# Gate and up of a feed-forward layer by Strassen's identity: seven block products in place of eight

## The chip, the cores and the metric

The kernel runs on one core of one Trainium2 chip. A core has TensorE (PE in the rows: matrix products, SBUF to PSUM), VectorE (DVE), ScalarE (ACT), GpSimd (POOL) and SyncE (SP, which issues most DMAs); each works through its own instructions in order, and they wait for one another by semaphores. The metric is the device time of one execution in microseconds.

## The reference, cut to what matters

All data are float32. 1024 tokens (32 x 32) of width 1024 go through three steps, each added to `x`: a readout over a context, causal attention with 16 heads, and the feed-forward layer, which is the one that the change touches:

```python
def _L0_ffn_ref(x, w_gate, w_up, w_down):          # w_gate, w_up: 4096 x 1024, w_down: 1024 x 4096
    gate = jnp.einsum('bsd,hd->bsh', x, w_gate)
    up = jnp.einsum('bsd,hd->bsh', x, w_up)
    gated = jax.nn.silu(gate) * up
    return jnp.einsum('bsh,dh->bsd', gated, w_down)
x = x + _L0_xattn_ref(_layernorm(x, axis=-1), ctx_2048, mask_BxS2_bk0)
x = x + _L0_attn_ref(_layernorm(x, axis=-1), L0_attn_Wq, L0_attn_Wk, L0_attn_Wv, L0_attn_Wo)
x = x + _L0_ffn_ref(_layernorm(x, axis=-1), L0_ffn_w_gate, L0_ffn_w_up, L0_ffn_w_down)
```

## The kernel before

**Split numbers.** TensorE multiplies in the type float32r, which keeps fewer bits than float32. So each operand is kept as two tensors: a high part, a copy of the raw numbers rounded to float32r (ScalarE, line 382 for weights, 513 for the hidden values), and a low part, raw minus high (GpSimd, line 300 for weights; VectorE, line 1128 for the hidden values). `three` (lines 524 to 526) makes of one product three matmuls, high by high, high by low and low by high, added up in one bank of PSUM. PSUM has eight banks `ps[:, 0..7, :]` of 512 columns.

**The feed-forward stage.** The 4096 hidden channels are done in `NC` = 16 chunks of 256, two tiles `k` of 128. The normalised tokens lie transposed in `xT_hi/xT_lo[half]`, 512 tokens each, as 8 slices of 128 inputs. In chunk `c`, TensorE first makes gate and up: for each `k` and each half a `gate_up`, which is two `job`s (gate, up), each 8 slices by three matmuls of 128x128 weights on 512 tokens; 8 jobs, 192 matmuls. Then `down`: 16 results (8 token tiles by 2 output halves `i`), each two `three`s, in bank `i % 8`; 96 matmuls. So a chunk has 288 matmuls of 512 columns.

**The other engines in a chunk.** For each of the four pairs of gate and up: ScalarE makes the Silu (line 511) from PSUM into `xn[0]`, VectorE multiplies by up (line 1125), ScalarE makes `h_hi` (513), VectorE `h_lo` (1128). VectorE adds each of the 16 results of `down` to `x` (line 1136). Three pairs of weight tiles of 128x2048 a chunk (two of gate and up, one of down) come by SyncE's queue into `raw[0..2]` and are split by ScalarE and GpSimd. Chunk 0 is written out ahead of a hardware loop over chunks 1 to 15. All orders are written by hand; nothing is scheduled.

**What sets the order.** `down` of a chunk waits for `h_ready` (three of the four hidden parts, then the fourth at i = 8), for `split_done[2]` and, from i = 8, for `down_added`, the additions that free its banks; `gate_up` of the next chunk waits for additions 10 to 16. At the end, rows of `x` go out as they are added up.

## Time and profile before

| | us |
|---|---|
| median of 3 runs | 1671.94 (1670.84 to 1674.14) |
| the profiled execution | 1671.12 |
| its span, first to last instruction | 1669.3 |
| TensorE busy in the span | 1632.6 (98%) |
| VectorE / ScalarE / GpSimd busy | 576.1 / 352.1 / 311.2 |
| feed-forward stage, TensorE from its first matmul of `down` in chunk 0 to the end | 664.3 to 1665.4 |

The span is cut by stage with the timeline: context readout to about 180 us, attention to about 630 us, the feed-forward stage from there. TensorE's granted clock was 0.998 of full speed. A TensorE row of the profile lasts 0.39 us while the next starts 0.23 us later, since matmuls are pipelined; the distance between starts is what a matmul costs.

### The profile page before, as it was taken

Reading aid. Unit: us, or ns where it says so; the run is one execution under the profiler, and the core shown is the slowest. Engines: PE = TensorE matmul, PEld = TensorE weight load, DVE = VectorE, ACT = ScalarE, POOL = GpSimd, SP = SyncE. Lnnn points to the kernel's source line nnn. Section 1 sums busy time; section 2 is a strip of 40 time slices with the busy share of each in tenths; the row PEclk is TensorE's granted clock in tenths of the full one; section 3 lists DMA queues with packets and bytes.
Section 4 is the critical chain, followed back from the end, with each engine's and each line's share of the span. In section 5 each row is a group of like instructions: output and inputs, shape, how many; then the busy total and the mean of one; then the engine's idle time right before and its main releaser. Section 6 shows DMA issues by size and latency. Waiting matters only on the chain.

```text
span 1669.3 us, 21252 instructions
## 1 busy us (share of the span) xinstructions
PE 1632.6 (98%) x8744; PEld 1348.5 (81%) x8744; DVE 576.1 (35%) x1115; ACT 352.1 (21%) x684; POOL 311.2 (19%) x133
## 2 busy tenths in 40 slices
PE   6999899999999999999999999999999999999999
PEld 5766688888888878888888888888888888888887
DVE  5666335153261683231321322312303313213223
ACT  3335312132221333121121121121111211211210
POOL 0000221212212121231231221211312312312110
PEclk9999999999999999999999999999999999999999
DMA  9662310101101001120111101201201201101002
GB/s 359 248 269 89 116 51 27 50 25 41 60 25 51 1 26 51 51 76 25 50 62 38 50 28 47 75 25 50 75 25 50 75 25 50 50 32 68 25 0 101
DMA packets 21205, 110.40 MB, mean 66 GB/s; under 512 B 2384, under 2 KB 2512, under 8 KB 12976
## 3 DMA queue, kind: packets, MB, share of 16 engines
q1 hardware_dynamic: 20736, 109.06, 17.8%
q10 hardware_dynamic: 432, 0.82, 0.2%
q8 instruction: 27, 0.44, 0.1%
q14 instruction: 10, 0.08, 0.0%
HBM read 105.68 MB, written 4.19 MB: 66 GB/s over the span
## 4 chain that ended last, share of the span: by engine, by line
PE 93%; DVE 4%; ACT 1%; DMA 1%; issue 1%; SPq 0%; POOL 0%; DVEq 0%
PE ps L524 27%; PE ps L526 27%; PE ps L525 27%; PE ps L555 3%; PE ps L602 2%; PE ps L578 1%; PE ps L730 1%; PE ps L530 1%; DMA x<-in_x 1%; ACT att_p L447 1%; DVE att L1060 1%; DVE att_z L1075 1%; PE ps L565 1%; PE ps L680 1%; DVE x L1095 0%
## 5 line engine op out<-in xcount | busy, mean ns | idle before, releaser
L524 PE MATMUL ps<-xT_hi,w_hi 128*128 128x512 f32 x1280 | 499.6, 390 | 0.0
L526 PE MATMUL ps<-xT_hi,w_lo 128*128 128x512 f32 x1280 | 498.2, 389 | 0.0
L525 PE MATMUL ps<-xT_lo,w_hi 128*128 128x512 f32 x1280 | 498.0, 389 | 0.0
L300 POOL TENSOR_TENSOR w_lo<-raw,w_hi 128x2048 fp32r<-128x2048 f32 x63 | 289.5, 4605 | 1087.3 <-ACT w_hi L382 1087.3
L526 PEld LDWEIGHTS ps<-xT_hi,w_lo 128*128 128x128 f32 x1280 | 240.3, 188 | 50.0
L524 PEld LDWEIGHTS ps<-xT_hi,w_hi 128*128 128x128 f32 x1280 | 240.3, 188 | 49.7 <-DVE w_lo L1100 0.5
L525 PEld LDWEIGHTS ps<-xT_lo,w_hi 128*128 128x128 f32 x1280 | 240.4, 188 | 49.4
L1125 DVE TENSOR_TENSOR xn<-xn,ps 128x512 f32<-128x512 f32 x64 | 44.0, 688 | 573.8 <-ACT xn L511 573.8
L1136 DVE TENSOR_TENSOR x<-ps,x 128x512 f32<-128x512 f32 x256 | 175.5, 691 | 143.1 <-PE ps L526 143.1
L511 ACT ACTIVATE xn<-ps 128x512 f32<-128x512 f32 x64 | 38.3, 599 | 796.1 <-PE ps L526 796.1
L525 PE MATMUL ps<-w_lo,h_hi 128*128 128x512 f32 x512 | 199.2, 389 | 0.0
L524 PE MATMUL ps<-w_hi,h_hi 128*128 128x512 f32 x512 | 199.2, 389 | 0.0
L526 PE MATMUL ps<-w_hi,h_lo 128*128 128x512 f32 x512 | 199.2, 389 | 0.0
L382 ACT ACTIVATE w_hi<-raw 128x2048 fp32r<-128x2048 f32 x64 | 120.4, 1903 | 103.6 <-PE ps L526 103.6
L525 PEld LDWEIGHTS ps<-w_lo,h_hi 128*128 128x128 f32 x512 | 96.1, 188 | 20.0
L526 PEld LDWEIGHTS ps<-w_hi,h_lo 128*128 128x128 f32 x512 | 96.1, 188 | 19.9
L524 PEld LDWEIGHTS ps<-w_hi,h_hi 128*128 128x128 f32 x512 | 96.1, 188 | 19.9
L524 PE MATMUL ps<-w_hi,xT_hi 128*128 128x256 f32 x256 | 75.2, 294 | 0.0
L526 PE MATMUL ps<-w_hi,xT_lo 128*128 128x256 f32 x256 | 72.4, 283 | 0.0
L525 PE MATMUL ps<-w_lo,xT_hi 128*128 128x256 f32 x256 | 72.4, 283 | 0.0
L555 PE MATMUL ps<-ident,ctx 128*128 128x128 f32 x512 | 62.8, 280 | 4.4 <-DMA ctx<-in_ctx 3.1
L555 PEld LDWEIGHTS ps<-ident,ctx 128*128 128x128 f32 x512 | 58.6, 145 | 8.3 <-DMA ctx<-in_ctx 3.5
(100 smaller groups left out, 1302.1 us busy)
## 6 DMA issues: line engine op xcount, KB each, us to landing
raw<-in_w SPq DMA_DIRECT2D x64, 1024.0 KB, 4.8
ctx<-in_ctx SPq DMA_DIRECT2D x64, 512.0 KB, 9.5
x<-in_x SPq DMA_DIRECT2D x8, 512.0 KB, 4.0
out<-x SPq DMA_DIRECT2D x8, 512.0 KB, 2.6
xn<-in_ext ACTq DMA_DIRECT2D x3, 128.0 KB, 8.2
mask<-in_mask ACTq DMA_DIRECT2D x1, 288.0 KB, 7.1
extT<-in_ext_t ACTq DMA_DIRECT2D x1, 128.0 KB, 4.8
```

Of the source, the lines that this page charges most:

```text
L300: pool.tensor_tensor(w_lo[wslot][:, :], raw[slot][:, :], w_hi[wslot][:, :].bitcast(F32), ALU.subtract).then_inc(split_done[slot], 1)
L382: act.activation(w_hi[wslot][:, :], raw[slot][:, :], ACT.Copy).then_inc(hi_done, 1)
L447: ins = act.activation(att_p[st % 2][:, h, :], rowsof[:, h * S:(h + 1) * S], ACT.Exp, bias=att_neg[st % 2][:, h:h + 1], accum_out=att_sum[ ...
L511: act.activation(sg(half), ps[:, 2 * n, :], ACT.Silu).then_inc(silu_done, 1)
L524: pe.matmul(dst, stat[0], moving[0], start=start, stop=False)
L525: pe.matmul(dst, stat[0], moving[1], start=False, stop=False)
L526: return pe.matmul(dst, stat[1], moving[0], start=False, stop=stop)
L530: mm = pe.transpose(ps[:, banks + k // 4, (k % 4) * P:(k % 4 + 1) * P], src[:, k * P:(k + 1) * P], ident[:, :])
L555: mm = pe.transpose(ps[:, b, e * MB + m * P:e * MB + (m + 1) * P], ctx[t % RING][:, b, j // 2, m, at:at + P], ident[:, :])
L602: pe.matmul(ps[q, RO + h, :], pT[:, m, q], ctx[t % RING][:, b, h, m, :], start=(m == 0), stop=False, skip_group_check=True)
L1125: dve.tensor_tensor(gf(half), sg(half), ps[:, 2 * n + 1, :], ALU.mult)\
L1136: dve.tensor_tensor(part, ps[:, i % 8, :], part, ALU.add).then_inc(down_added, 1)
```

## The change

Chunk 0 stays as it is. From chunk 1 on, gate and up are each one `unit`. The weights of a unit are cut as a 2x2 matrix of blocks A11, A12, A21, A22 (128 channels x 512 inputs), the tokens as a 2x2 matrix B11, B12, B21, B22 (512 inputs x 512 tokens). Strassen's identity, in Winograd's form, gives the four results C from seven block products:

| place | weight side | token side | bank |
|---|---|---|---|
| 0 | A11 | B11 | 4 |
| 1 | S1 = A21 + A22 | T1 = B12 - B11 | 6 |
| 2 | S2 = S1 - A11 | T2 = B22 - T1 | 4, added up |
| 3 | A12 | B21 | 5 |
| 4 | S3 = A11 - A21 | T3 = B22 - B12 | 4, added up |
| 5 | A22 | T4 = B21 - T2 | 7 |
| 6 | S4 = A12 - S2 | B22 | 6, added up |

Each product is 4 slices by three matmuls, 12 matmuls of 512 columns. The running sum in bank 4 is copied out by ScalarE after places 0, 2 and 4 (`keep`, into `kept[0..2]`), and VectorE adds a kept sum to a bank (`gather`); for up, it writes that sum back to PSUM and then multiplies by the Silu of gate. `down` has its 96 matmuls as before, over halves first and token tiles second, and the first four results begin with their `k` = 0 part.

The four token-side sums T are made once, by VectorE in chunk 0, between the work that it has there: 10 tensor additions of 128x2048, both inputs in SBUF, and 4 low parts of the same size (`combine`, `turned_sum_lo`); ScalarE makes the 4 high parts. The weight-side sums S are made in each chunk by GpSimd, 4 a unit. Weights now come as 12 blocks of 128x512 a chunk (256 KB each) into six slots, and GpSimd makes 18 low parts of 128x512 a chunk (14 products, 4 blocks of down) in a ring of six, each after ScalarE's high part; the slot of block n + 6 is free when product n is done. Rows of `x` go out in 16 pieces in place of 8.

What TensorE waits for in a chunk c from 1 on: place 0 of gate for addition 13 of the chunk before, place 1 for addition 15, place 3 for all 16; each product for its block's low part; places 1, 2, 4 and 5 in chunk 1 for the sums T1 (`t_ready` 2), T2 (3), T3 (1) and T4 (4); places 2 and 4 for the copy of bank 4 before them; place 6 of up for the sum read out of bank 6. `down` begins when the first hidden part is ready, takes its `k` = 1 parts of results 0 to 3 when three are, results 4 on when all four are, and from result 8 on waits for addition i - 7. In chunk 0, VectorE's list after the third hidden part is: low part of T3, fourth hidden part, first half of T1, additions 1 and 2, second half of T1, additions 3 and 4, T1 joined, additions 5 to 7, low part of T1, additions 8 to 10, first half of T4, additions 11 to 13, T4 joined, additions 14 to 16, low parts of T2 and T4.

The core of the diff, in the order GpSimd, ScalarE, TensorE, VectorE in chunk 0, VectorE in the loop; `round_after(n)` makes the high part of block n + 6, `finish_part` the Silu of gate or `h_hi`:

```diff
--- before.py
+++ after.py
+BLK = 512
+RAW_BLOCKS, RAW_SLOTS = 12, 6
+BLOCKS, PRODUCTS, BLOCK_SLOTS = 18, 14, 6
+ADDS = 2 * NT
...
+            def unit(c, u):
+                a11, a21, a22, a12 = [blk[raw_of(u, i)] for i in range(4)]
...
+                pool.tensor_tensor(s_sum[:, :], a21[:, :], a22[:, :], ALU.add).then_inc(sum_done, 1)
+                block_split(c, 7 * u, a11)
+                block_split(c, 7 * u + 1, s_sum)
+                pool.wait_ge(block_lo, (c - 1) * BLOCKS + (7 * u + 2))
+                pool.tensor_tensor(s_sum[:, :], s_sum[:, :], a11[:, :], ALU.subtract).then_inc(sum_done, 1)
+                pool.tensor_tensor(a21[:, :], a11[:, :], a21[:, :], ALU.subtract).then_inc(sum_done, 1)
+                block_split(c, 7 * u + 2, s_sum)
+                block_split(c, 7 * u + 3, a12)
...
+            def keep(c, u, i):
+                act.wait_ge(product_done, (c - 1) * PRODUCTS + (7 * u + 2 * i + 1))
...
+                act.activation(kept[i][:, :], ps[:, Y, :], ACT.Copy).then_inc(part_kept, 1)
...
+                for u in range(2):
+                    for place in range(7):
+                        if place in (0, 2, 4):
+                            keep(c, u, place // 2)
+                        round_after(7 * u + place)
+                        if place >= 3:
+                            finish_part(c, u, place - 3)
+                for n in range(14, BLOCKS):
+                    round_after(n)
...
             with pe.Fori(1, NC) as c:
-                for k in range(2):
-                    pe.wait_ge(split_done[k], c + (ATT_USES + 1))
-                    for half in range(2):
-                        gate_up(c, k, half)
-                down(c)
+                unit(c, 0)
+                unit(c, 1)
+                add_hidden(c)
...
+            first_hidden(0)
+            dve.wait_ge(split_done[0], ATT_USES + 1)
+            combine(raw[0][:, :], b22[0], b12[0], ALU.subtract)
+            combine(raw[1][:, :], b22[1], b12[1], ALU.subtract)
+            combined()
+            combine(raw[1][:, :], raw[1][:, :], raw[0][:, :], ALU.add, raw=True)
+            first_hidden(1)
...
+            combine(t2_raw[:, :], raw[1][:, :], b11[0], ALU.add)
+            combined()
+            combine(t2_raw[:, :], t2_raw[:, :], b11[1], ALU.add, raw=True)
+            first_hidden(2)
+            turned_sum_lo(1, t3_lo[:, :], raw[1][:, :], t3_hi[:, :])
+            first_hidden(3)
+            combine(t1_top[:, :], b12[0], b11[0], ALU.subtract)
+            first_add(0, 2)
+            combine(t1_raw[:, :], b12[1], b11[1], ALU.subtract)
+            first_add(2, 4)
...
             with dve.Fori(1, NC) as c:
-                chunk(c)
+                for i in range(4):
+                    gather(c, 0, i)
+                gather(c, 1, 0)
+                gather(c, 1, 1)
+                low(c, 0)
+                gather(c, 1, 2)
+                low(c, 1)
+                low(c, 2)
+                gather(c, 1, 3)
+                low(c, 3)
+                for i in range(ADDS):
```

How it moves instructions is seen best at three places. **VectorE in chunk 0**, from the first hidden part on (`raw`, `t_raw`, `t_lo` hold sums of tokens). Before:

```order
L1125 TENSOR_TENSOR xn1<-xn0,ps 128x512 [waits silu_done]
L1128 TENSOR_TENSOR h_lo<-xn1,h_hi 128x512 [waits h_hi_done]
L1125 TENSOR_TENSOR xn1<-xn0,ps 128x512 [waits silu_done]
L1128 TENSOR_TENSOR h_lo<-xn1,h_hi 128x512 [waits h_hi_done]
L1125 TENSOR_TENSOR xn1<-xn0,ps 128x512 [waits silu_done]
L1128 TENSOR_TENSOR h_lo<-xn1,h_hi 128x512 [waits h_hi_done]
```

Now:

```order
L1387 TENSOR_TENSOR xn1<-xn0,ps 128x512 [waits silu_done]
L1389 TENSOR_TENSOR h_lo<-xn1,h_hi 128x512 [waits h_hi_done]
L1411 TENSOR_TENSOR raw0<-xT_hi1 128x2048 [waits split_done0]
L1411 TENSOR_TENSOR raw1<-xT_lo1 128x2048
L1411 TENSOR_TENSOR raw1<-raw1,raw0 128x2048 [waits t_own]
L1387 TENSOR_TENSOR xn1<-xn0,ps 128x512 [waits silu_done]
L1389 TENSOR_TENSOR h_lo<-xn1,h_hi 128x512 [waits h_hi_done]
L1411 TENSOR_TENSOR t2_raw_51<-raw1,xT_hi0 128x2048 [waits t_raw,gu_done]
L1411 TENSOR_TENSOR t2_raw_51<-t2_raw_51,xT_lo0 128x2048 [waits t_own]
L1387 TENSOR_TENSOR xn1<-xn0,ps 128x512 [waits silu_done]
L1389 TENSOR_TENSOR h_lo<-xn1,h_hi 128x512 [waits h_hi_done]
```

Three additions of 128x2048 stand ahead of the second hidden part, and two between the second and the third. **VectorE in the loop**, where the last hidden parts are made. Before:

```order
L1124 REGISTER_ALU
L1125 TENSOR_TENSOR xn1<-xn0,ps 128x512 [waits silu_done]
L1128 TENSOR_TENSOR h_lo<-xn1,h_hi 128x512 [waits h_hi_done]
L1133 ISA
L1135 ISA [waits down_done]
```

Now:

```order
L1476 TENSOR_TENSOR hid_77<-ps,hid_77 128x512 [waits gate_silu,up_added]
L1480 TENSOR_TENSOR h_lo<-hid_77,h_hi 128x512 [waits hid_hi] x2
L1466 REGISTER_ALU
L1471 TENSOR_TENSOR ps<-ps,kept1_75 128x512 [waits product_done]
L1473 REGISTER_ALU
L1476 TENSOR_TENSOR hid_77<-ps,hid_77 128x512 [waits gate_silu,up_added]
L1480 TENSOR_TENSOR h_lo<-hid_77,h_hi 128x512 [waits hid_hi]
```

Between the last product and the last hidden part there are now a sum, a product and a low part, and two low parts may stand ahead of them. **GpSimd in the loop.** Before:

```order
L300 TENSOR_TENSOR w_lo1<-raw1,w_hi1 128x2048 [waits hi_done]
L299 REGISTER_ALU
L300 TENSOR_TENSOR w_lo2<-raw2,w_hi2 128x2048 [waits hi_done]
L299 REGISTER_ALU
L300 TENSOR_TENSOR w_lo0<-raw0,w_hi0 128x2048 [waits hi_done]
```

Now, the first part of the first unit:

```order
L449 TENSOR_TENSOR s_sum_73<-blk1_68,blk2_69 128x512 [waits blk_full2,blk_full1,blk_full0]
L438 REGISTER_ALU
L440 TENSOR_TENSOR b_lo0_61<-blk0_67,b_hi0_55 128x512 [waits block_hi]
L438 REGISTER_ALU
L440 TENSOR_TENSOR b_lo1_62<-s_sum_73,b_hi1_56 128x512 [waits block_hi]
L453 TENSOR_TENSOR s_sum_73<-s_sum_73,blk0_67 128x512 [waits block_lo]
L454 TENSOR_TENSOR blk1_68<-blk0_67,blk1_68 128x512
L438 REGISTER_ALU
L440 TENSOR_TENSOR b_lo2_63<-s_sum_73,b_hi2_57 128x512 [waits block_hi]
```

Three long instructions a chunk have become 26 short ones, of which 8 are sums that ScalarE's high parts wait for.

## Rows read from the trace of the kernel before

**Rows 1.** the page: span and instructions, and the busy time of the engines (part 1)

```profile
span 1669.3 us, 21252 instructions
...
PE 1632.6 (98%) x8744; PEld 1348.5 (81%) x8744; DVE 576.1 (35%) x1115; ACT 352.1 (21%) x684; POOL 311.2 (19%) x133
```

**Rows 2.** busy time of each engine by stretch, of one whole chunk

```profile
core 0: us, PE busy (x) PEld busy (x) DVE busy (x) ACT busy (x) POOL busy (x), PEclk, DMA share, GB/s
...
697.10:762.40 65.30, 65.30 (x289) 54.09 (x289) 16.41 (x24) 10.34 (x11) 13.78 (x3) 1.00 0.14 48
```

**Rows 3.** groups of TensorE from 664 us on: out<-in, shapes, count | busy us, mean ns

```profile
L526 PE MATMUL ps<-xT_hi,w_lo 128*128 128x512 f32 x961 | 373.8, 389 | 0.0
...
L526 PE MATMUL ps<-w_hi,h_lo 128*128 128x512 f32 x512 | 199.2, 389 | 0.0
```

**Rows 4.** timeline of TensorE where chunk 0 goes over to down: start us, us

```profile
664.06 0.39 PE L526 MATMUL ps<-xT_hi,w_lo 128*128 128x512 f32 x1
664.29 0.39 PE L524 MATMUL ps<-w_hi,h_hi 128*128 128x512 f32 x1
```

**Rows 5.** timeline of VectorE, the first product of gate and up in chunks 1 and 2

```profile
697.76 0.69 DVE L1125 TENSOR_TENSOR xn<-xn,ps 128x512 f32<-128x512 f32 x1 [10.82 <-ACT xn L511]
...
763.04 0.69 DVE L1125 TENSOR_TENSOR xn<-xn,ps 128x512 f32<-128x512 f32 x1 [10.73 <-ACT xn L511]
```

**Rows 6.** groups of VectorE by shape

```profile
L1136 DVE TENSOR_TENSOR x<-ps,x 128x512 f32<-128x512 f32 x256 | 175.5, 691 | 143.1 <-PE ps L526 143.1
L1128 DVE TENSOR_TENSOR h_lo<-xn,h_hi 128x512 fp32r<-128x512 f32 x64 | 47.0, 734 | 44.7 <-ACT h_hi L513 44.7
L1125 DVE TENSOR_TENSOR xn<-xn,ps 128x512 f32<-128x512 f32 x64 | 44.0, 688 | 573.8 <-ACT xn L511 573.8
...
L1100 DVE TENSOR_TENSOR w_lo<-raw,w_hi 128x2048 fp32r<-128x2048 f32 x1 | 2.3, 2293 | 0.7 <-ACT w_hi L382 0.7
```

**Rows 7.** groups of GpSimd by shape

```profile
L300 POOL TENSOR_TENSOR w_lo<-raw,w_hi 128x2048 fp32r<-128x2048 f32 x63 | 289.5, 4605 | 1087.3 <-ACT w_hi L382 1087.3
...
L292 POOL TENSOR_TENSOR shift<-mean_var,rstd 128x1 f32<-128x1 f32 x16 | 3.0, 190 | 1.3
```

**Rows 8.** groups of ScalarE by shape

```profile
L382 ACT ACTIVATE w_hi<-raw 128x2048 fp32r<-128x2048 f32 x64 | 120.4, 1903 | 103.6 <-PE ps L526 103.6
...
L513 ACT ACTIVATE h_hi<-xn 128x512 fp32r<-128x512 f32 x64 | 40.5, 632 | 48.2 <-DVE xn L1125 48.2
...
L511 ACT ACTIVATE xn<-ps 128x512 f32<-128x512 f32 x64 | 38.3, 599 | 796.1 <-PE ps L526 796.1
...
L511 ACT ACT_TABLE_LOAD x1 | 1.3, 1283 | 0.0
```

**Rows 9.** timeline of VectorE in chunk 0

```profile
641.63 0.69 DVE L1128 TENSOR_TENSOR h_lo<-xn,h_hi 128x512 fp32r<-128x512 f32 x1 [0.70 <-ACT h_hi L513]
654.24 0.69 DVE L1125 TENSOR_TENSOR xn<-xn,ps 128x512 f32<-128x512 f32 x1 [11.92 <-ACT xn L511]
655.63 0.69 DVE L1128 TENSOR_TENSOR h_lo<-xn,h_hi 128x512 fp32r<-128x512 f32 x1 [0.70 <-ACT h_hi L513]
...
659.30 3.35 DVE L1128 TENSOR_TENSOR h_lo<-xn,h_hi 128x512 fp32r<-128x512 f32 x1 [0.70 <-ACT h_hi L513]
...
668.57 0.69 DVE L1136 TENSOR_TENSOR x<-ps,x 128x512 f32<-128x512 f32 x1 [0.17 <-PE ps L526]
```

**Rows 10.** timeline of GpSimd in chunk 0

```profile
657.48 4.61 POOL L300 TENSOR_TENSOR w_lo<-raw,w_hi 128x2048 fp32r<-128x2048 f32 x1 [24.12 <-ACT w_hi L382]
668.36 9.19 POOL L300 TENSOR_TENSOR w_lo<-raw,w_hi 128x2048 fp32r<-128x2048 f32 x2 [6.26 <-ACT w_hi L382]
```

**Rows 11.** DMA issues: out<-in, queue, count, KB each, median us to landing

```profile
raw<-in_w SPq DMA_DIRECT2D x64, 1024.0 KB, 4.8
```

**Rows 12.** timeline of VectorE, the last addition of the program

```profile
1665.54 0.69 DVE L1136 TENSOR_TENSOR x<-ps,x 128x512 f32<-128x512 f32 x1 [0.67 <-PE ps L526]
```

More of the change, by code:

```diff
@@ L264, in _, with blocks @@
-            sync.wait_ge(stored, 16 * NT)
+            for i in range(FFN_SLOTS):
+                sync.wait_ge(split_done[i], ATT_USES)
+                sync.dma_start(raw[i][:, :], w_in[ATT_PAIRS + i]).then_inc(raw_full[i], 16)
+            def blocks(c, first, last):
+                for j in range(first, last):
+                    slot = j % RAW_SLOTS
+                    sync.dma_start(blk[slot][:, :], block_in[(c - 1) * RAW_BLOCKS + j])\
+                        .then_inc(blk_full[slot], 16)
@@ L516, in _, with first_hidden, turned_sum_hi @@
-            chunk(0, first=True)
+            def first_hidden(n):
+                k, half = n // 2, n % 2
+                act.wait_ge(gu_done, 3 if n == 1 else n + 1)
+                act.activation(sg(half), ps[:, 2 * n, :], ACT.Silu).then_inc(silu_done, 1)
+                act.wait_ge(h_done, n + 1)
+                act.activation(h_hi[:, k, half * HALF:(half + 1) * HALF], gf(half), ACT.Copy)\
+                    .then_inc(h_hi_done, 1)
+            def turned_sum_hi(n, dst, src):
+                act.wait_ge(t_raw, n)
+                act.activation(dst, src, ACT.Copy).then_inc(t_hi_done, 1)
@@ new lines, in finish_part, with chunk, round_after @@
+            def finish_part(c, u, i):
+                act.wait_ge(c_done, (c - 1) * 8 + (4 * u + i + 1))
+                here = hidden(hid, PARTS[i])
+                if u == 0:
+                    act.activation(here, here, ACT.Silu).then_inc(gate_silu, 1)
+                else:
+                    act.activation(hidden(h_hi, PARTS[i]), here, ACT.Copy).then_inc(hid_hi, 1)
+            def chunk(c, last=False):
+                def round_after(n):
+                    if not last or n + BLOCK_SLOTS < BLOCKS:
+                        next_round(c, n + BLOCK_SLOTS)
+                for u in range(2):
+                    for place in range(7):
[6 more added lines that the diff above has]
+                    round_after(n)
@@ L1139, in _, with b_side, combine @@
-            with dve.Fori(1, NC) as c:
-                chunk(c)
+            inputs = (slice(0, 4), slice(4, 8))
+            def b_side(half, j):
+                return (flat(xT_hi[half][:, inputs[j], :]).bitcast(F32),
+                        flat(xT_lo[half][:, inputs[j], :]).bitcast(F32))
+            b11, b21 = b_side(0, 0), b_side(0, 1)
+            b12, b22 = b_side(1, 0), b_side(1, 1)
+            step = [0]
+            def combine(dst, one, other, op, raw=False):
+                ins = dve.tensor_tensor(dst, one, other, op)
+                if raw:
+                    ins.then_inc(t_raw, 1)
+                else:
+                    ins.then_inc(t_own, 1)
+                    step[0] += 1
```

333 lines of the change are left out of this document (277 added, 56 removed).

## The prediction

> **What bounds the kernel now.** The page says that TensorE is busy 98% of the span [rows 1]. Busy time alone doesn't say whether anything else could set the pace, so I read the feed-forward stage by itself. In the list of waits from 664 us on, TensorE has no entry: no other engine holds it up there. The window of one chunk shows the same: 65.30 us long, TensorE busy all of it, VectorE 16.4 us, ScalarE 10.3, GpSimd 13.8 [rows 2]. So the stage is a row of matmuls end to end, and its time is their number times their distance. A matmul of 512 columns lasts 0.389 us in the groups [rows 3] but they overlap: the next starts 0.23 us later [rows 4]. The exact distance comes from the chunk period: the same VectorE instruction starts at 697.76 and at 763.04 [rows 5], 65.28 us apart, and 288 matmuls lie between: 0.2267 us each. The granted clock of that window is 1.00, the upper level (2.4 GHz).
>
> **What is removed.** In each of 15 chunks the 8 jobs of 24 matmuls become 14 products of 12: 192 become 168, and `down` keeps 96. 24 x 0.2267 = 5.44 us a chunk, 81.6 us in all. The new matmuls have the old shape and read both operands from SBUF as before, so I give them the same distance; a chunk is then 264 x 0.2267 = 59.84 us and a product 2.72 us. All of it is on the path, as long as TensorE goes on waiting for nothing. So the rest is a search for new waits.
>
> **GpSimd in a chunk.** 18 low parts and 8 sums of 128x512. The trace has no such size. Its 128x2048 instruction takes 4.605 us and a one-column one 0.19 us [rows 7]. A quarter of 4.605 is 1.15 us; with the one-column time as fixed cost it is 0.19 + 4.415/4 = 1.29 us. I take 1.29: 26 x 1.29 = 33.5 us of 59.84. Not the bound by rate.
>
> **ScalarE and VectorE in a chunk.** ScalarE: 18 high parts, 6 copies of bank 4, 4 Silus, 4 high hidden parts, each about 0.60 to 0.63 [rows 8]: 20 us. The Silu's table is loaded once and the copies between bring no other load [rows 8], so the new order of Silus and copies costs none. VectorE: 4 sums for gate, 8 instructions for up, 4 low parts, 16 additions, 32 x 0.69 [rows 6] = 22 us. Neither is a bound by rate.
>
> **The ring of blocks.** Block n + 6 may be split when product n is done, and is needed 5 products, 13.6 us, later. Its chain is one high part (0.63) and one low part (1.29), and where a sum stands before, up to two sums more: 0.63 + 3 x 1.29 = 4.5 us. The longest queue is at the start of a chunk, when blocks 4 and 5 come free with the end of `down`: ScalarE 1.3 us, GpSimd 1.3 us behind for each, both ready after 3.2 us and needed after 10.9. GpSimd then runs on: block 6 at 5.2, sum, block 7 at 7.8, block 8 at 10.7, two sums to 13.3, block 9 at 14.6, needed at 24.5. So all blocks have 7 us or more to spare. The raw blocks are 256 KB; a 1024 KB load lands in 4.8 us [rows 11], and each is asked for at least 8 us before its first use. I cost ring and loads at nothing; the cover is these 7 us.
>
> **Banks within a unit.** Place 2 adds to bank 4 after its copy: product 0 ends, one product (2.72) follows, the copy takes 0.60. Place 6 of gate needs a copy and a sum, 0.60 + 0.69 and the handovers, against 2.72. Handovers are small: in chunk 0 multiply to low part takes 1.39 us (654.24 to 655.63), of which 0.69 and 0.63 are work [rows 6, 8, 9], so two cost 0.07. ScalarE works in order, and its high part of block 9 waits for GpSimd's sum until 12.0; the copy after product 4 is due at 13.6. Cost nothing, with 1.4 us to spare: this is the thinnest place inside a unit.
>
> **The start of down.** Count from the end of the last product. VectorE did the third part's sum and product from -2.72 to -1.34, low parts 2 and 3 to about 0.1; sum and product of the fourth to 1.5; ScalarE's high part to 2.2; low part to 2.9. TensorE has the first 24 matmuls of `down`, 5.44 us, before it asks for it. Hidden by 2.5 us, if VectorE's instructions take 0.69. They need not: the low part at 659.30 took 3.35 us instead of 0.69 [rows 9], and ended 0.56 us after GpSimd's w_lo (657.48 to 662.09) [rows 10]. The addition at 668.57, with one input in PSUM, took 0.69 while GpSimd's next one ran [rows 9, 10]. So VectorE with both inputs in SBUF stands still while GpSimd works; with one in PSUM it doesn't. Each of the three low parts after the sums can wait for one GpSimd instruction, now 1.29 long: worst 2.9 + 3.9 = 6.8, 1.4 us late. By my count of GpSimd's list, it works at -2 to 0 and 0.6 to 4.5, so one or two are hit: 4.2 to 5.5 against 5.44. I take nothing and keep 1.4 x 15 = 21 us as the upper bound.
>
> The Trainium skill, "SBUF — State Buffer", section "Who interferes with whom", has the rule behind this row: a VectorE instruction with two SBUF inputs and a GpSimd one that reads SBUF exclude each other for the whole instruction, whoever came first. The row agrees for VectorE's side; no row shows GpSimd being held, which would be the difference between 2.2 and 3.3 us in the next part.
>
> **Chunk 0, once.** VectorE gets 14 instructions of 128x2048, both inputs in SBUF, 2.29 us each [rows 6]: 32 us into a chunk in which `down` and place 0 wait for its additions. Walk it with the old times. Hidden part 1 is done at 642.3 [rows 9]; T3 takes to 649.3, before part 2 begins at 654.24. That ends at 656.3 and T2's first half runs to 658.6. GpSimd's w_lo starts at 657.48 [rows 10] or, if it is held out too, at 658.6, and ends at 662.1 or 663.2. T2's second half waits for that and then takes 2.3, hidden part 3 another 2.05: ready at 666.5 or 667.6. `down` started at 664.29 [rows 4]. A first wait of 2.2 or 3.3 us; I take 3.3, the one that holds both ways. Then T3's low part to 669.8, hidden part 4 to 671.8, and the list of sums and additions: 13 additions by 692.2 (5 long ones, 11.5, and 13 of 0.69, 9.0), 15 by 695.9 (one more long, two short), T2's low part by 698.9. TensorE ends `down` at 667.6 + 21.8 = 689.4, waits for addition 13 to 692.2, ends place 0 at 694.9, waits for addition 15 to 695.9, ends place 1 at 698.6 and waits for T2 to 698.9. Without any of it, place 2 would start at 664.3 + 21.8 + 5.4 = 691.5. So 7.4 us, 6.3 with the smaller first wait. On top GpSimd starts on chunk 1's blocks at 671.8, and 8 of its instructions fall into this stretch; each may hold VectorE for up to 1.29: 0 to 10.3 us. The 15 additions between aren't held, and GpSimd itself pauses for ScalarE, so not every one meets: I take 3, two or three meetings. Chunk 0 costs 10.4, bounds 6.3 and 17.7.
>
> **The end.** The last addition starts at 1665.54 [rows 12]; 256 KB go out after it instead of 512. Nothing.
>
> **Sum** against the profiled execution: span 1669.3 - 81.6 + 10.4 = 1598.1; 1.8 us lie around the span (1671.12 - 1669.3), so 1599.9; the median is 0.8 above that execution: 1600.7, say 1601. Bounds: 1671.9 - 81.6 + 6.3 = 1596.6 and 1671.9 - 81.6 + 17.7 + 21 = 1629.
>
> **Rivals.**
> *A wait at each start of down, or at another thin place of the unit.* For it: the 3.35 us row and margins of 1.4 and about 0 to 2.5 us. Against: one low part in 64 was hit before (their mean of 0.734 is 0.69 and that one, 2.66/64) [rows 6], and with short GpSimd instructions each hit is small. 1601 + 7 to 21: 1608 to 1629; a second thin place would add as much, up to 1645.
> *The chain of ScalarE and GpSimd is slower than its rates.* Each engine waits in order for the other, and register arithmetic for the waits stands between. If a block's turn costs more than 2.3 us instead of 1.29 plus handover (59.84/26), the ring sets the period: at 2.4 us, 62.4 us a chunk, 1601 + 15 x 2.6 = 1640.
> *Slower than before: GpSimd becomes the pace by a fixed cost of its short instructions.* One mechanism, in `block_split` and the sums. The period must pass 65.28 less a fifteenth of chunk 0's cost, 64.6 us: 2.48 us an instruction, 1.3 more than a quarter of the long one. At 2.7 the chunk is 70.2 and the time 1672 + 10 + 15 x 4.9 = 1756. For it: no row of this size. Against: 0.19 us for one column [rows 7] leaves no room for a fixed cost of 1.3.
> *It does nothing to the bound*, if matmuls into banks shared between products kept a larger distance: 264 at 0.247 us would give the old period. Against: the matmul at 664.29 is the first of `down`, in another bank than the one at 664.06, and follows at 0.23 us like any other [rows 4].
>
> **How the numbers follow.** Forecast, 1596 to 1608: 0.62. Wait at each start of down: 0.22. Slow chain: 0.08. Slower: 0.04. No effect: 0.01. Better than my lower bound, if TensorE's chunk 0 waits overlap: 0.03. The range 1595 to 1629 leaves out 0.16 or so. A measurement here tells about 0.2%, 3.3 us, from no change. Faster: 0.95; same 0.01; slower 0.04.
>
> **What would show it.** TensorE's count falls by 360 to 8384 and its distance stays 0.2267: the same VectorE row in two chunks lies 59.8 us apart. GpSimd's 512-wide instruction reads 1.15 to 1.3 us. The waits of TensorE list `h_lo` or T2 in chunk 0 only, some 10 us in all; if they list `h_lo` 15 times, the first rival is right; if `b_lo`, the ring. Low parts (L1480) of more than 0.7 us beside GpSimd show the hold. The prediction is wrong if the period is above 60.5 or chunk 0 costs more than 18.

## The result, and the profile after

The changed kernel takes 1599.57 us, the median of 4 runs (1599.30 to 1599.82), against 1672.95 us before in the same session (4 runs, 1670.84 to 1674.14). The ratio is 0.9566, with a 95% interval of 0.9554 to 0.9578: faster by 4.3%, and 1.4 us below the predicted 1601.

The page of the changed kernel answers to [rows 1]: the span is shorter, TensorE's count lower by 360, and the three other engines do more.

```profile
span 1598.0 us, 23260 instructions
...
PE 1556.2 (97%) x8384; PEld 1282.9 (80%) x8384; DVE 710.2 (44%) x1249; ACT 489.5 (31%) x1003; POOL 626.5 (39%) x478
```

The window of one whole chunk answers to [rows 2]. It is 59.84 us long, TensorE is busy in all of it, and the window takes in one matmul more than the chunk's 264. GpSimd is the next busiest, with 33.9 us; the prediction had reckoned 33.5.

```profile
core 0: us, PE busy (x) PEld busy (x) DVE busy (x) ACT busy (x) POOL busy (x), PEclk, DMA share, GB/s
767.20:827.04 59.84, 59.84 (x265) 49.55 (x265) 23.18 (x32) 19.02 (x32) 33.92 (x27) 1.00 0.19 53
```

VectorE's timeline answers to [rows 5]: its first gather of chunk 2 and of chunk 3 start exactly 59.84 us apart.

```profile
767.90 0.69 DVE L1468 TENSOR_TENSOR hid<-ps,kept 128x512 f32<-128x512 f32 x1 [10.10 <-PE ps L1086]
...
827.74 0.69 DVE L1468 TENSOR_TENSOR hid<-ps,kept 128x512 f32<-128x512 f32 x1 [10.10 <-PE ps L1086]
```

TensorE's waits from 625 us to the end (columns: the line that waits, what for, us in total, times, longest) are few, and none lies behind 720 us. The entry "issue" is the first matmul of `down` in chunk 0.

```profile
PE ps L717 <- issue: 2.8, 1, 2.8
PE ps L1086 <- DVE hid L1468: 2.0, 1, 2.0
PE ps L1086 <- DVE x L1397: 1.4, 2, 0.9
```

The groups of the new work, from 720 us on for GpSimd and from 697 us on for VectorE (count | busy us, mean ns | idle before), show the 128x512 instruction of GpSimd that no row of before had (1.29 to 1.30 us in four of GpSimd's six groups; 1.34 in the low parts of sums and 1.52 in the sums of line 454, which can meet VectorE's low parts), and the low parts of the hidden tile, which are slower than the 0.69 us of other VectorE instructions of this size [rows 6].

```profile
L440 POOL TENSOR_TENSOR b_lo<-blk,b_hi 128x512 fp32r<-128x512 f32 x172 | 221.6, 1292 | 205.5 <-ACT b_hi L654 205.5
...
L1480 DVE TENSOR_TENSOR h_lo<-hid,h_hi 128x512 fp32r<-128x512 f32 x60 | 66.2, 1121 | 10.6 <-ACT h_hi L676 10.5
L1471 DVE TENSOR_TENSOR ps<-ps,kept 128x512 f32<-128x512 f32 x60 | 41.5, 692 | 181.7 <-PE ps L1086 152.9 <-ACT kept L668 28.9
```

**Where the time went.** I count a stage that hides differences upstream: from the start of the last gate/up matmul of chunk 0 to the start of the last matmul of the program. (The matmul that starts the stage lies between 663.65 and 667.26 us in the profiles of this text, and nearly all of that difference is there before the attention stage begins; see the kernel called mended.) Before, the stage is 1665.02 - 664.06 = 1000.96 us; after, 1594.36 - 664.09 = 930.27. It lost 70.7 us: 81.6 removed, 10.9 paid in the transition from chunk 0 to 1. The span lost 71.3 (1669.3 to 1598.0): the other 0.6 us lie behind the last matmul, 4.3 us from its start to the end of the span before and 3.7 now, with 256 KB in place of 512 to go out last. The rest of this text is about these 10.9 us, and about how near the steady chunk is to paying too.

### The profile page after: what moved, and what is told of

Its sections match the earlier page's. It is cut to its first block, busy times and chain, and to the rows that moved or that the text cites. A ratio compares the mean times of both kernels' runs of the same rounds, so it can differ in the third digit from the quotient of the medians.

```text
span 1598.0 us, 23260 instructions
## 1 busy us (share of the span) xinstructions
PE 1556.2 (97%) x8384; PEld 1282.9 (80%) x8384; DVE 710.2 (44%) x1249; ACT 489.5 (31%) x1003; POOL 626.5 (39%) x478
## 4 chain that ended last, share of the span: by engine, by line
PE 89%; DVE 7%; ACT 1%; DMA 1%; issue 1%; POOL 1%; SPq 0%; DVEq 0%; ACTq 0%; POOLq 0%
PE ps L1086 35%; PE ps L717 14%; PE ps L719 14%; PE ps L718 14%; PE ps L748 3%; PE ps L795 2%; PE ps L771 2%; PE ps L923 1%; DVE t_raw L1411 1%; PE ps L723 1%; DMA x<-in_x 1%; ACT att_p L583 1%; DVE att L1324 1%; DVE att_z L1339 1%; PE ps L758 1%
## 5 line engine op out<-in xcount | busy, mean ns | idle before, releaser
L440 POOL TENSOR_TENSOR b_lo<-blk,b_hi 128x512 fp32r<-128x512 f32 x180 | 239.5, 1334 | 211.8 <-ACT b_hi L654 211.8
L409 POOL TENSOR_TENSOR w_lo<-raw,w_hi 128x2048 fp32r<-128x2048 f32 x18 | 83.5, 4640 | 325.8 <-ACT w_hi L518 325.8
L1086 PE MATMUL ps<-xT_hi,b_hi 128*128 128x512 f32 x480 | 187.8, 391 | 3.5 <-DVE hid L1468 2.0
L1086 PE MATMUL ps<-xT_lo,b_hi 128*128 128x512 f32 x480 | 187.5, 391 | 0.0
L1086 PE MATMUL ps<-xT_hi,b_lo 128*128 128x512 f32 x480 | 187.3, 390 | 0.0
L717 PE MATMUL ps<-b_hi,h_hi 128*128 128x512 f32 x480 | 186.7, 389 | 0.0
L718 PE MATMUL ps<-b_lo,h_hi 128*128 128x512 f32 x480 | 186.7, 389 | 0.0
L717 PE MATMUL ps<-xT_hi,w_hi 128*128 128x512 f32 x320 | 126.2, 394 | 0.0
L719 PE MATMUL ps<-xT_hi,w_lo 128*128 128x512 f32 x320 | 124.7, 390 | 0.0
L718 PE MATMUL ps<-xT_lo,w_hi 128*128 128x512 f32 x320 | 124.6, 389 | 0.0
```

The source lines that it names most:

```text
L409: pool.tensor_tensor(w_lo[wslot][:, :], raw[slot][:, :], w_hi[wslot][:, :].bitcast(F32), ALU.subtract).then_inc(split_done[slot], 1)
L440: pool.tensor_tensor(b_lo[slot][:, :], src[:, :], b_hi[slot][:, :].bitcast(F32), ALU.subtract).then_inc(block_lo, 1)
L717: pe.matmul(dst, stat[0], moving[0], start=start, stop=False)
L718: pe.matmul(dst, stat[0], moving[1], start=False, stop=False)
L719: return pe.matmul(dst, stat[1], moving[0], start=False, stop=stop)
L1086: mm = pe.matmul(ps[:, bank, :], stat[a], moving[b], start=first and m == 0, stop=(s == 3 and m == 2), skip_group_check=True)
```

## The transition from chunk 0 to chunk 1, in the trace

TensorE's timeline at the first wait (start us, us) shows two things. The matmul after 664.09 starts 2.92 us late. And from the fourth matmul on, at 668.01, the distance is 0.43 us, eight times; it is back at 0.23 from 671.41 on.

```profile
664.09 0.39 PE L719 MATMUL ps<-xT_hi,w_lo 128*128 128x512 f32 x1
667.24 0.47 PE L717 MATMUL ps<-w_hi,h_hi 128*128 128x512 f32 x1 [2.76 <-issue]
...
668.42 0.63 PE L718 MATMUL ps<-w_lo,h_hi 128*128 128x512 f32 x1
668.85 0.63 PE L719 MATMUL ps<-w_hi,h_lo 128*128 128x512 f32 x1
...
671.41 0.40 PE L719 MATMUL ps<-w_hi,h_lo 128*128 128x512 f32 x1
671.65 0.40 PE L717 MATMUL ps<-w_hi,h_hi 128*128 128x512 f32 x1
```

The windows of this stretch and of the one behind the wait at 711.55 have a granted clock (third from the end) of 0.60 and 0.61: most of each ran at the lower of the two levels, 1.2 of 2.4 GHz. TensorE was busy all through both; before each it had waited.

```profile
667.20:671.40 4.20, 4.16 (x11) 3.30 (x12) 3.50 (x4) 2.65 (x4) 0.00 (x0) 0.60 0.02 4
711.50:715.70 4.20, 4.15 (x11) 3.26 (x12) 0.59 (x1) 1.67 (x3) 3.79 (x4) 0.61 0.17 61
```

The first wait is VectorE's. Its timeline and GpSimd's of chunk 0:

```profile
656.26 2.28 DVE L1411 TENSOR_TENSOR t_raw<-raw,xT_hi 128x2048 f32<-128x2048 f32 x1
658.58 6.57 DVE L1411 TENSOR_TENSOR t_raw<-t_raw,xT_lo 128x2048 f32<-128x2048 f32 x1
665.08 0.68 DVE L1387 TENSOR_TENSOR xn<-xn,ps 128x512 f32<-128x512 f32 x1
```

```profile
657.51 5.49 POOL L409 TENSOR_TENSOR w_lo<-raw,w_hi 128x2048 fp32r<-128x2048 f32 x1 [24.10 <-ACT w_hi L518]
...
671.67 3.01 POOL L449 TENSOR_TENSOR s_sum<-blk,blk 128x512 f32<-128x512 f32 x1 [8.67 <-DVE h_lo L1389]
674.65 3.43 POOL L440 TENSOR_TENSOR b_lo<-blk,b_hi 128x512 fp32r<-128x512 f32 x1
```

The profile names no releaser for this wait ("issue"); it is the third hidden part, whose low part VectorE ends at 667.14 (666.45 and 0.69 us), and the matmul starts at 667.24. GpSimd's `w_lo` takes 5.49 us instead of 4.64, the mean of the 18 of its kind: it stood until VectorE's first half of T2 was done at 658.5. Then it held T2's second half until 663.0, and that took 6.57 us instead of 2.28. Each holds the other, and the one that comes first works. This is the side that no row of before showed. It goes on at 671.67: there GpSimd's instructions of 1.29 us take 3.0 to 3.4 beside VectorE's long sums, while these keep to 2.28 or go up to 2.8. So GpSimd arrives late in chunk 1, and ScalarE too, whose T4 high part (694.13) stands ahead of blocks 4 and 5:

```profile
694.13 1.92 ACT L640 ACTIVATE w_hi<-t_raw 128x2048 fp32r<-128x2048 f32 x1 [10.03 <-DVE t_raw L1411]
695.95 1.14 ACT L654 ACTIVATE b_hi<-blk 128x512 fp32r<-128x512 f32 x2
...
709.13 0.63 ACT L654 ACTIVATE b_hi<-s_sum 128x512 fp32r<-128x512 f32 x1 [3.25 <-POOL s_sum L453]
709.67 0.61 ACT L674 ACTIVATE hid<-hid 128x512 f32<-128x512 f32 x1
710.19 0.58 ACT L668 ACTIVATE kept<-ps 128x512 f32<-128x512 f32 x1
```

`down` ended at 690.8 and blocks 4 and 5 came free with it, yet ScalarE began on them at 695.95. GpSimd's sum 2 is then ready at 709.1, ScalarE's high part and copy wait in order behind it, VectorE gathers at 710.80, and place 6 of gate starts at 711.55, 2.21 us late. (The list of TensorE's waits in the section on the change leaves this one out: place 6 of gate waits for VectorE's second gather, which reads bank 6 and the copy made after place 4.)

```profile
710.80 1.29 DVE L1468 TENSOR_TENSOR hid<-ps,kept 128x512 f32<-128x512 f32 x2 [6.01 <-ACT kept L668]
711.55 0.50 PE L1086 MATMUL ps<-xT_hi,b_hi 128*128 128x512 f32 x1 [2.05 <-DVE hid L1468]
```

GpSimd's lateness has two sources here. ScalarE gave it blocks 4 and 5 some 5 us after `down` ended, and then the two low parts took 5.90 us (from 696.64) instead of 2.6, beside VectorE's low parts of T2 and T4. The theory is thus: the 10.9 us are VectorE's list (places 0 to 2) and ScalarE's order (place 6), with the clock on top. The rival: they come with the new form itself, and the steady chunk pays as well, unseen.

## Experiments

All ratios are to the kernel before on the same chip; "stage" is the length defined above, and the last column is the stage less the 930.27 us of the changed kernel. The changed kernel itself was run again only beside mended, gp3 and plain_down; elsewhere the medians hold differences that arise ahead of the stage, so the stage is what is compared.

| kernel | median us | ratio, 95% interval | stage us | against after |
|---|---|---|---|---|
| eight | 1678.09 | 1.0034, 1.0021 to 1.0046 | 1007.90 | +77.6 |
| w2_early | 1598.59 | 0.9549, 0.9533 to 0.9565 | 927.65 | -2.6 |
| hi45_early | 1598.35 | 0.9552, 0.9536 to 0.9568 | 926.86 | -3.4 |
| both | 1596.87 | 0.9546, 0.9530 to 0.9562 | 924.26 | -6.0 |
| after_again | 1600.94 | 0.9574, 0.9560 to 0.9587 | 930.27 | 0 |
| mended | 1593.54 | 0.9531, 0.9518 to 0.9544 | 922.78 | -7.5 |
| mended_again | 1595.28 | 0.9541, 0.9528 to 0.9554 | 922.78 | -7.5 |
| late_t4 | 1593.80 | 0.9534, 0.9521 to 0.9547 | 922.78 | -7.5 |
| gp1 | 1603.13 | 0.9592, 0.9577 to 0.9607 | 932.59 | +2.3 |
| gp2 | 1620.65 | 0.9695, 0.9680 to 0.9710 | 950.34 | +20.1 |
| gp3 | 1654.39 | 0.9891, 0.9876 to 0.9906 | 983.71 | +53.4 |
| plain_down | 1623.81 | 0.9714, 0.9699 to 0.9729 | 954.19 | +23.9 |

### Is it the number of products? (eight)

```diff
-                    for s in range(4):
+                    for s in [0, 1, 2, 3] * (2 if place == 3 else 1):
```

> Place 3 of each unit, which starts its bank afresh, is computed twice: eight products in place of seven, 24 more matmuls a chunk, everything else as in the changed kernel. Theory (the stage is a row of matmuls and the whole gain is the matmuls left out): 15 x 24 x 0.2267 = 81.6 us more, 1599.6 + 81.6 = 1681, with the same waits of TensorE in chunks 0 and 1, and so some 8 to 11 us above the kernel before, which is the price of the token sums. Rival (part of the gain is from something else in the rewrite, such as the new order of down or the smaller loads): the time comes out clearly below or above 1681.

With an eighth product in each unit the gain is gone: the time is 0.3% above before, and 3 us below the expected 1681. The stage is 77.6 us longer than in the changed kernel, not 81.6: the two more products a chunk cost 81.6, and 4.0 come back, since the wait at place 6 in chunk 1 and the slow stretch behind it are gone (place 3 gives ScalarE and GpSimd 2.7 us more). The period is that of before [rows 5], 65.28 us, with all the new work beside TensorE's; VectorE's first gather in two chunks:

```profile
774.70 0.69 DVE L1468 TENSOR_TENSOR hid<-ps,kept 128x512 f32<-128x512 f32 x1 [12.82 <-PE ps L1086]
...
839.98 0.69 DVE L1468 TENSOR_TENSOR hid<-ps,kept 128x512 f32<-128x512 f32 x1 [12.82 <-PE ps L1086]
```

So the new operations on the other engines cost TensorE nothing in the steady chunk, and the 24 matmuls are the whole gain there.

### The first wait (w2_early)

```diff
             first_hidden(0)
+            weights(2, ATT_USES, 2)
             turned_sum_hi(1, t3_hi[:, :], raw[1][:, :])
             first_hidden(1)
-            weights(2, ATT_USES, 2)
```

> ScalarE makes the high part of chunk 0's down weights ahead of that of T3, so GpSimd's w_lo of 4.6 us falls where VectorE is idle later (it stood idle 5.2 us before the second hidden part), and no longer into T2. Theory (the first wait of TensorE, 2.9 us, and the 1.2 GHz stretch behind it come from GpSimd's w_lo holding VectorE's second half of T2 for 4.3 us): that half takes 2.3 us, down starts without a wait, no matmuls at a distance of 0.43 us follow, VectorE's list ends about 4 us earlier; place 2 of chunk 1 starts 3.8 us earlier: 1595.8. Rival (VectorE's list alone is too long and the hold only hides in it): the waits move to place 0 and the time stays within 1 us.

The first wait shrank from 2.9 to 0.3 us, so its cause was GpSimd's `w_lo` beside T2. The gain was 2.6 us, not 3.8 (and the median 1598.59, not 1595.8: `down` started 2.9 us later than in the first profile, for what lies ahead of it). VectorE's timeline shows why: the hold moved to T3 (6.69 us at 647.38), and then hidden part 1 came late, because ScalarE now had T3's high part in front of its Silu. The stretch at the lower clock, which I had expected to go, didn't; it moved behind a wait of 2.31 us at place 0 (granted clock 0.59 from 692.0 to 696.2), where its 1.7 us took the place of the waits at places 1 and 2.

```profile
647.38 6.69 DVE L1411 TENSOR_TENSOR raw<-xT_lo 128x2048 f32<-128x2048 f32 x1
654.11 2.29 DVE L1411 TENSOR_TENSOR raw<-raw 128x2048 f32<-128x2048 f32 x1
658.87 0.69 DVE L1387 TENSOR_TENSOR xn<-xn,ps 128x512 f32<-128x512 f32 x1 [2.47 <-ACT xn L633]
```

### Place 6 of gate in chunk 1 (hi45_early, both)

```diff
-            turned_sum_hi(4, w_hi[1][:, :], t4_raw[:, :])
             act.wait_ge(down_done, ADDS)
             block_round(1, 4)
             block_round(1, 5)
+            turned_sum_hi(4, w_hi[1][:, :], t4_raw[:, :])
```

> ScalarE makes the high parts of blocks 4 and 5 of chunk 1 ahead of that of T4 instead of behind it. Theory (TensorE's wait of 2.2 us at place 6 of gate in chunk 1 is GpSimd running late, held by the low parts of T2 and T4, with ScalarE's copy of bank 4 queued behind the sum that GpSimd is late with): GpSimd's two low parts start up to 5 us earlier, the wait at place 6 and the 1.2 GHz stretch behind it go: 2.2 + about 1.9 us, 1595.5. Rival (GpSimd is held by VectorE just the same and stays late): the wait stays, 1599.6.

> Both reorderings of ScalarE's list together. Theory: the gains add, 1599.6 - 3.8 - 4.1 = 1591.7, and no stretch at the lower clock is left in the feed-forward stage. Rival (they compete for the same slack): about 1595.5.

GpSimd starts on blocks 4 and 5 4.8 us earlier, counted from the start of the stage, and the wait at place 6 and its slow stretch are gone: -3.4 us (2.21 + 0.10 + 1.56 = 3.9 saved, 0.5 of it lost again at place 2). GpSimd is still held by VectorE's low parts of T2 and T4 (4.59 us for two that need 2.6); but it starts early enough for that. So ScalarE's order is shown to be a cause; the hold was not taken away alone, and without it GpSimd would have been 3.3 us earlier, an estimate from the rows above, which could have covered the wait as well.

The two edits together give -6.0, exactly the sum, so their gains are separate. But I had expected 1591.7 and no slow stretch, and neither came: 1596.87, a stage 1.9 us longer than -3.8 - 4.1 would give, and a stretch at the lower clock (0.58 from 692.3 to 696.4) behind a wait of 2.31 us at place 0. It cost nothing more, since place 2 waited for VectorE's low part of T2 even so (0.26 us).

### ScalarE's order mended (after_again, mended)

```diff
             first_hidden(0)
-            turned_sum_hi(1, t3_hi[:, :], raw[1][:, :])
-            first_hidden(1)
             weights(2, ATT_USES, 2)
+            first_hidden(1)
+            turned_sum_hi(1, t3_hi[:, :], raw[1][:, :])
             first_hidden(2)
```

(and the edit of hi45_early)

> The changed kernel, unchanged, as the base for the three kernels beside it: about 1599.6 us; its feed-forward stage, from the first matmul of down in chunk 0 to the last matmul, 930.3 us as in the first trace.

> ScalarE prepares block 2 of chunk 0 and the hidden part 1 before the high part of the sum T3, and blocks 4 and 5 of chunk 1 before the high part of T4. Theory: with T3's high part behind hidden part 1, hidden part 2 is no longer 1.9 us late as in w2_early, so the gain there is 3.8 us and not 2.6; with the 3.4 of hi45_early the stage is 7.3 to 7.9 us shorter than in the changed kernel, 922.4 to 923.0 us, the whole time about 1593.5. Rival: VectorE's list in chunk 0 is bound by something else than ScalarE's order (its long sums beside GpSimd's w_lo), and the stage is that of the kernel called both, 924.3 us, the whole time about 1595.5.

As the theory had it: 922.78 us, inside 922.4 to 923.0, and not the 924.26 of both. No first wait, no wait at place 6, no slow stretch in the stage. What is left of TensorE's waits is VectorE's list:

```profile
PE ps L1086 <- DVE x L1397: 2.0, 2, 1.1
PE ps L1086 <- DVE w_lo L1423: 0.5, 1, 0.5
```

On one chip the medians are 1593.54 and 1600.94: 7.4 us or 0.5% below the changed kernel, and the intervals of the two ratios, 0.9518 to 0.9544 and 0.9560 to 0.9587, don't meet. mended_again, on another chip and in another session, has 1595.28 with the same stage to 0.01 us. Its profiled execution took 1592.10 us and that of mended 1593.77, and the 1.67 us between them lie ahead of `down` (its first matmul starts at 664.08 and at 665.76). They are lost in the context readout, where TensorE's granted clock from 20 to 30 us (third from the end) was 1.00 in mended_again and 0.83 in mended; from 30 us on every matmul of mended is 1.6 to 1.7 us behind:

```profile
20.00:30.00 10.00, 8.25 (x75) 5.87 (x74) 8.33 (x11) 2.67 (x6) 0.55 (x1) 0.83 1.03 408
```

The profiles of w2_early, hi45_early, both and eight, in which `down` starts latest, have 0.66 to 0.69 in that window, and the kernel before and the changed kernel 1.00.

### The last three microseconds (late_t4, mended_again)

The difference to mended, ScalarE's list first:

```diff
                         round_after(7 * u + place)
+                        if isinstance(c, int) and c == 1 and u == 0 and place == 2:
+                            turned_sum_hi(4, w_hi[1][:, :], t4_raw[:, :])
...
-            turned_sum_hi(4, w_hi[1][:, :], t4_raw[:, :])
...
-            first_add(7, 10)
+            first_add(7, 13)
             combine(t4_raw[:, :], b21[0], t2_raw[:, :], ALU.subtract)
-            first_add(10, 13)
-            combined()
-            combine(t4_raw[:, :], t4_raw[:, :], b21[1], ALU.add, raw=True)
             first_add(13, 16)
             turned_sum_lo(2, w_lo[0][:, :], t2_raw[:, :], w_hi[0][:, :])
+            combined()
+            combine(t4_raw[:, :], t4_raw[:, :], b21[1], ALU.add, raw=True)
```

> The kernel called mended, with the sum T4 made later in the transition from chunk 0 to 1: its first half behind the 13th addition, its second half behind T2's low part, its high part on ScalarE behind the high part of block 8 in chunk 1. What is left in mended's transition is three waits on VectorE's list (the 13th and 15th addition, T2's low part), 3.0 us. Theory (VectorE's list ahead of places 0 to 2 is the bound, and each long sum in it counts 2.8 us): two long sums leave the list ahead of the additions and one ahead of T2's low part, so all three waits go but for some 0.2 us, 2.5 to 3 us faster than mended, about 1591. Rival (T4 is now too late for place 5, or its high part makes ScalarE and so GpSimd late, as in gp3): the waits come back at place 5 or 6 of gate in chunk 1, no gain or up to 3 us slower than mended.

> The kernel called mended once more, on the chip of late_t4, as its base: 1593.5 us, stage as before.

The rival was right: no gain. The waits at places 0 to 2 went, and others came at places 5 and 6 of gate in chunk 1. That the two stages agree to 0.01 us is chance as far as the trace shows, since the waits are different ones:

```profile
PE ps L1088 <- DVE w_lo L1425: 2.2, 1, 2.2
PE ps L1088 <- DVE hid L1469: 0.5, 1, 0.5
```

VectorE then stood 5.15 us for T4's high part, which I had put behind the high part of block 8, and that waited for GpSimd's sum until 696.97 (the low part that VectorE makes next):

```profile
699.45 2.29 DVE L1425 TENSOR_TENSOR w_lo<-t_raw,w_hi 128x2048 fp32r<-128x2048 f32 x1 [5.15 <-ACT w_hi L640]
```

T4's high part ahead of block 8 was not tried.

### How near is the steady chunk to a wait? (gp3, gp1, gp2)

```diff
                 slot = n % BLOCK_SLOTS
+                for k in range(3 if n == 8 else 0):
+                    pool.tensor_tensor(b_lo[slot][:, :], src[:, :], b_hi[slot][:, :].bitcast(F32),
+                                       ALU.subtract).then_inc(again, 1)
+                    pool.wait_ge(again, (c - 1) * 3 + (k + 1))
```

(gp1 and gp2: 1 and 2 in place of 3)

> GpSimd computes the low part of block 8 three more times in every chunk, the same values again, each behind a wait for the one before: some 1.37 us each, 4.1 us a chunk. GpSimd stays far from full (37.6 of 59.8 us). Theory (the thinnest place of a unit is ScalarE's copy after product 4, which stands in order behind the high part of block 9 and so behind GpSimd's sum; it has some 1.4 us to spare): place 6 of gate waits about 2.2 us in every chunk from 2 on, 15 times 2.2 = 33 us, and up to 1.6 us more each time if TensorE's clock falls behind the wait as in chunk 1, so 33 to 57 us slower than the changed kernel, with TensorE's waits listed at VectorE's hid. Rival (the ring of blocks with its 7 us to spare is what counts, and copies don't hang on it): no difference.

> As gp3, with one extra low part of block 8 a chunk instead of three (1.37 us). From gp3: three of them, 4.1 us, made place 6 of gate wait 2.4 us in every chunk, so ScalarE's copy after product 4 has 1.7 us to spare in the steady chunk (the prediction reckoned 1.4). Theory: 1.37 us fits into it, so no wait in the steady chunk and a time within 2 us of the changed kernel's 1600; only chunk 1, which waits 2.2 us already, waits 1.4 us longer. Rival (the cost goes with GpSimd's work, 54 us for three repeats, 18 us for one): about 1618.

> As gp3, with two extra low parts of block 8 a chunk (2.74 us). Theory: 1.0 us beyond the spare 1.7, so place 6 of gate waits 1.0 to 1.1 us in each chunk, 15 to 17 us in all, 1616 to 1618. Rival (the cost goes with GpSimd's work): 36 us, about 1636.

gp3: 4.1 us more on GpSimd a chunk made TensorE wait in all 15 chunks, at the place named, for VectorE's gather behind ScalarE's copy. GpSimd was idle for 40% of the chunk all the while (37.7 us busy in the chunk from 845.0 to 907.4). These are GpSimd's three repeats, ScalarE's queue behind them, and the waits of TensorE from 720 us on, 14 of 2.28 us (2.43 us from start to start, beyond the usual distance):

```profile
836.03 4.01 POOL L442 TENSOR_TENSOR b_lo<-s_sum,b_hi 128x512 fp32r<-128x512 f32 x3 [1.48 <-ACT b_hi L659]
840.12 1.29 POOL L445 TENSOR_TENSOR b_lo<-s_sum,b_hi 128x512 fp32r<-128x512 f32 x1
841.48 1.29 POOL L458 TENSOR_TENSOR s_sum<-s_sum,blk 128x512 f32<-128x512 f32 x1
```

```profile
842.81 0.63 ACT L659 ACTIVATE b_hi<-s_sum 128x512 fp32r<-128x512 f32 x1 [6.86 <-POOL s_sum L458]
843.35 0.61 ACT L679 ACTIVATE hid<-hid 128x512 f32<-128x512 f32 x1
843.87 0.58 ACT L673 ACTIVATE kept<-ps 128x512 f32<-128x512 f32 x1
```

```profile
PE ps L1091 <- DVE hid L1473: 31.9, 14, 2.3
```

gp2: 2.74 us more, a gap of 1.06 us in each of the 14 later chunks (12.6 us in the list of waits). gp1: 1.37 us more, no wait behind chunk 1, and 2.3 us more in chunk 1, which was late already. That is 1.3 us of wait, near the 1.4 expected, and 1 us at the lower clock, which I hadn't counted; the median, 1603.13, is 3 us above 1600 and not within 2. The spare time of ScalarE's copy follows twice: 4.09 - 2.43 = 1.66 us from gp3, 2.74 - 1.06 = 1.68 from gp2. The prediction had 1.4. The rival "the cost goes with GpSimd's work" is out: 2.3, 20.1 and 53.4 us aren't 1 : 2 : 3. I missed gp2 by 3 us (15 to 17 us of cost expected, 20.1 measured) and gp3's 53.4 lies at the upper end. The part that I had left out of gp2 is chunk 1's own (7.2 us there against 3.9); the period of the other 14 is 1.19 us longer, 1.06 and some 0.1 at the matmul behind the wait.

### Do the held low parts cost nothing? (plain_down)

```diff
-                for i in range(4):
-                    down_part(c, i, 0, True)
                 pe.wait_ge(block_lo, (c - 1) * BLOCKS + 16)
                 pe.wait_ge(hid_ready, (c - 1) * 4 + 3)
                 for i in range(4):
+                    down_part(c, i, 0, True)
                     down_part(c, i, 1, False).then_inc(down_done, 1)
```

> The first four results of down take both hidden tiles at once, as before the change, and so need the third hidden part before the first matmul of the second tile instead of after all four of the first; the order of TensorE's matmuls changes, not their number. Theory: the third low part is ready at 796.36 in the steady chunk of the changed kernel and TensorE would ask for it at about 795.5 to 795.8: a wait of 0.5 to 1 us a chunk, 8 to 15 us in all, TensorE's waits listed at h_lo in every chunk; that would show that the held low parts (mean 1.12 us) cost nothing only because 24 matmuls cover them. Rival (the low parts are early enough anyway): no difference, and no wait.

A wait in each of the 15 chunks, for the low part of the hidden tile:

```profile
PE ps L717 <- DVE h_lo L1479: 19.2, 15, 1.4
```

It is 1.5 us a chunk from start to start (0.58 in the last one) and not 0.5 to 1, and 23.9 us in all and not 8 to 15; with the slower matmuls just behind each wait the period is 1.66 us longer. My error was in the reading: I took 795.5 as the time at which TensorE would ask, but in the changed kernel `down` starts at 794.90, and the third low part is ready at 796.36, 1.46 us behind. So the first 12 matmuls of `down` that need only the first hidden tile are worth 23.9 us here, a third of the gain.

## The prediction, point by point

**The removed matmuls: right.** 24 x 0.2267 x 15 = 81.6; the period is 59.84 to the hundredth, and eight shows that nothing else of the new form moves it. The rival by which the change would do nothing, a larger distance between matmuls, fell with the same row.

**GpSimd's instruction: right.** 1.29 us taken, 1.292 measured. The fixed cost plus a quarter of the rest was the right way, a quarter of the whole (1.15) wasn't. GpSimd as the pace, the rival that would have been slower than before, fell with this row: it was priced at 2.48 us an instruction. The slow chain fell with the period of 59.84.

**The ring: right.** No wait for `b_lo` anywhere.

**The start of down: nothing, right, with 0.9 us to spare.** By the prediction the fourth low part comes at 4.2 to 5.5 us, against 5.44. VectorE's timeline of chunk 2, in which `down` starts at 794.90:

```profile
791.63 1.06 DVE L1480 TENSOR_TENSOR h_lo<-hid,h_hi 128x512 fp32r<-128x512 f32 x1
...
793.95 2.41 DVE L1480 TENSOR_TENSOR h_lo<-hid,h_hi 128x512 fp32r<-128x512 f32 x2
...
798.39 1.04 DVE L1480 TENSOR_TENSOR h_lo<-hid,h_hi 128x512 fp32r<-128x512 f32 x1 [0.70 <-ACT h_hi L676]
```

Ready at 799.43, 4.5 us in, and asked for at 5.44: 0.9 us to spare. All four low parts were hit (a mean of 1.12 instead of 0.69), more than the one or two that I counted, but none for a whole instruction of GpSimd. The first rival's mechanism is there, then, and its price isn't: 12 more matmuls of cover take it, as plain_down shows from the other side. The gathers and products with one input in PSUM kept to 0.69, as read from before.

The Trainium skill, "SBUF — State Buffer", section "Who interferes with whom", says that the pair of ports that VectorE and GpSimd share is taken for the whole instruction and whoever issues first blocks the other. The trace now agrees both ways: 6.57 us for VectorE's sum, 5.49 and 3.4 us for GpSimd's.

**Inside a unit: right in the steady chunk, wrong in chunk 1.** "Cost nothing, with 1.4 us to spare" holds in chunks 2 to 15 (1.7 measured). The step that failed is that it was worked out for the steady chunk only. In chunk 1 GpSimd and ScalarE come late out of the transition, by more than the 1.7 us, and place 6 waits 2.2 us. The prediction had put that wait at nothing. With blocks 4 and 5 ahead of T4's high part in ScalarE's list it is gone (hi45_early).

**Chunk 0: 10.4 against 10.9, and that the sum is so near is luck: terms offset each other.** How late TensorE is against an undisturbed row of matmuls from 664.32 on:

| at | by the prediction | measured |
|---|---|---|
| first matmul of down | 3.3 | 2.9 |
| place 0 | 6.1 | 5.3 (starts 691.41) |
| place 1 | 7.1 | 6.5 (695.35) |
| place 2 | 7.4, and 3 for the hold | 6.8 (698.33) |
| end of place 6 of gate, on to the end | no more: 10.4 | 10.9 |

The walk of VectorE's list was good to 0.8 us, and of the two first waits, 2.2 and 3.3, the mechanism of the larger one was right, the hold both ways; the 2.9 us lie between the two. The 3 us for "two or three meetings" was mis-sized: VectorE's long instructions took 2.28 to 2.83 us instead of 2.29, some 2.5 us over in all, and the last of these lie behind place 2; in the same stretch GpSimd paid with 2 us a time. What this and ScalarE's order did to GpSimd is what I left out: it came back as place 6 in chunk 1, 2.3 us, and 1.6 of clock.

**The clock: not in the prediction.** Behind the first wait eight matmuls ran at the lower level, 1.6 us. That one cost nothing in the end: TensorE then reached place 0 later and waited 0.68 there, and in hi45_early, where it didn't fall, it waited 2.29 at the same place. Both times addition 13 sets when place 0 starts. The one behind place 6 cost its 1.6 us, since nothing comes behind it to absorb it.

**The end: nothing forecast, 0.6 us gained.** The last addition starts 0.51 us after the last matmul as before [rows 12]; 256 KB go out after it instead of 512, and the span ends 0.6 us sooner behind the last matmul. That is too little to be told from the median.

## What to carry over

Where TensorE is the pace, count its instructions and multiply by their start-to-start distance; the period here shrank by that product to a hundredth of a microsecond, and the gain is that times 15, less what the transition into the new form costs. Work out the transition with the list of every engine, and not only of the one that TensorE waits for next: what one engine loses there (here GpSimd, held by VectorE's long sums and served late by ScalarE) shows up later, on an engine that works in order behind it. And a free engine isn't a free chain: GpSimd was idle 40% of the time and 2.7 us more in the wrong place cost 20 us, so measure the spare time of each in-order queue by adding work until it hurts.
